# A graph network on one core: one wait a step for TensorE, relayed by ScalarE, and 32-bit step words

## The chip, the cores and the metric

The kernel runs on one core of one Trainium2 chip. The metric is the device time of one execution in microseconds. A core has TensorE (matmuls), VectorE, ScalarE and GpSimd for work on tiles, SyncE for transfers, and 16 DMA engines. In the profile they are PE, DVE, ACT, POOL and SP; a trailing q (PEq, PEldq, DVEq, SPq) marks the engine's instruction stream, that is waits, register work and DMA issues.

## What is computed

6250 nodes with 256 features, 100000 edges sorted by destination. Two blocks, each with a layer norm, a relu and a residual: a graph convolution of three hops, then a graph attention of two layers with four heads.

```python
h = relu(layernorm(x))
for i in range(3):                       # hops
    h = h * out_norm[:, None]
    h = segment_sum(h[src], dst, N)      # 100000 rows of 256 floats
    h = (h * in_norm[:, None]) @ W[i] + b[i]
    if i < 2: h = relu(h)
x = x + h
h = relu(layernorm(x))
for layer in range(2):                   # attention, with a loop edge at every node
    alpha = leaky_relu(a_src[src] + a_dst[dst])
    w = exp(alpha - segment_max(alpha, dst)[dst])
    h = segment_sum(w * h[src], dst) / segment_sum(w, dst)[dst] + bias
x = x + h
```

## The kernel before

The edges, in order of destination, are cut into EC = 782 chunks of 128. The nodes are cut into NT = 49 tiles of 128. A *step* is one chunk for one tile of destinations; a chunk that reaches into the next tile is used in two steps, so there are S = 832 steps. Which chunk and which tile belongs to a step depends on the data and is worked out on the chip at the start: `step_tab` holds, for each step, four 16-bit words: how many chunks must have arrived (ARRIVALS), the place of the chunk in the ring (SLOT_AT), the place of the tile's sums (SUMS_AT) and of its logits (LOGITS_OF). The helper `step_values` loads some of them into an engine's registers (the profile puts these loads on L363).

One hop is a pipeline of four engines, each with its stream of instructions in fixed order:

- GpSimd issues one indirect DMA for each chunk (L695), 128 rows of 1 KB from `conv_tab` into one of U = 64 slots of `ring`. Chunk c may go out when the step c - 15 has been multiplied (`products_done`, L694).
- SyncE waits for the chunks in order and counts them in `arrived` (L484, in `landed`).
- VectorE, in step s, makes the one-hot matrix of the step s + 3 from `dloc` (L1413, 128x128 f32, four buffers), then waits for the product of step s and adds it to the tile's sums in `acc` (L1421, in `accumulate`).
- TensorE, in step s, waits for the one-hots, for the add that frees the PSUM bank (four of them) and for the arrival of the chunk, and multiplies one-hot by rows (L1127). The fp32 matmul is two passes, with two records each of weight load and matmul. The two loads of eight words each, chunk counts and slots, stand ahead of every eighth step.

After a hop TensorE, ScalarE and VectorE multiply by W[i], and SyncE stores the next table. ScalarE has nothing to do within a hop, save that in hop 1 it sends the keys and the start and end flags of segments, which attention needs later, to DRAM and back (L805 to L817) while VectorE works on them in `flag_work`.

Attention goes over the same steps in groups of 16. TensorE and VectorE load sixteen words a group with `step_values`, and `accumulate` is shared with the hops.

## Time and profile before

| | |
|---|---|
| median of 3 runs | 6875.43 us (6857.97 to 6877.12) |
| the profiled execution | 6875.32 us, its span 6873.5 us |
| mean granted TensorE clock | 0.71 |
| TensorE busy (matmul) | 4202.8 us, 61% |
| VectorE busy | 3621.6 us, 53% |
| ScalarE busy | 2136.3 us, 31% |
| GpSimd busy | 4130.3 us, 60% |
| DMA | 625.46 MB, mean 91 GB/s |

Busy counts tile work alone; register loads and waits are not in it. The mean of a matmul record is modelled. An idle time that the profile puts on "issue" ended with nothing that it can name, and "remote" is a signal whose sender it does not know.

### The profile page before, as it was taken

How to read it: one execution, taken by the hardware profiler on the slowest of the kernel's cores; microseconds unless marked ns; L12 is line 12 of the kernel's file. 1: busy time of each engine (PE TensorE's matmuls, PEld its weight loads, DVE VectorE, ACT ScalarE, POOL GpSimd, SP SyncE). 2: the span in 40 equal slices, each digit the busy share in tenths (PEclk: the TensorE clock that was granted, in tenths of full speed). 3: DMA queues.
4: the chain of work that ended last, by engine and by line, in shares of the span. 5: the costliest groups of instructions: out<-in, count | busy, mean ns of one | idle time of the engine just before them, and what ended most of it. 6: DMA issues, size and time to landing. Idle time of an engine off the chain costs nothing. (4 is left out here: it accounts for less than half of the span.)

```text
span 6873.5 us, 84355 instructions
## 1 busy us (share of the span) xinstructions
PE 4202.8 (61%) x14997; PEld 2812.5 (41%) x14997; DVE 3621.6 (53%) x12180; ACT 2136.3 (31%) x7094; POOL 4130.3 (60%) x4276
## 2 busy tenths in 40 slices
PE   8555555565555556555555636666666556666774
PEld 7333333343333334333333424444444334444442
DVE  6444444544444444444444636666666556666667
ACT  4000000020000002000000247677777467767774
POOL 7666666366666664666666356566664556666663
PEclk7666666776666668666666867777778777777776
DMA  3333333133333332333333233333333323333334
GB/s 100 95 95 89 91 91 91 55 103 90 91 89 91 90 90 85 90 91 90 91 91 90 85 112 88 87 90 89 88 90 86 104 77 89 88 89 87 89 89 133
DMA packets 309602, 625.46 MB, mean 91 GB/s; under 512 B 85343, under 2 KB 180411, under 8 KB 309080
## 3 DMA queue, kind: packets, MB, share of 16 engines
q0 software_dynamic: 192928, 530.18, 27.7%
q1 hardware_dynamic: 109800, 88.51, 4.1%
q8 instruction: 167, 2.74, 0.2%
q10 hardware_dynamic: 6384, 1.39, 0.1%
q14 instruction: 323, 2.65, 0.1%
HBM read 573.23 MB, written 47.33 MB: 90 GB/s over the span
## 5 line engine op out<-in xcount | busy, mean ns | idle before, releaser
L1127 PE MATMUL main<-ring,oh 128*128 x4992 | 2039.7, 573 | 1582.9 <-DVE oh L1413 775.2
L695 POOL DMA_INDIRECT ring<-conv_tab,csrc x2346 | 2221.4, 947 | 1232.7 <-issue 613.0
L1421 DVE TENSOR_TENSOR acc<-acc,main 128x264 f32 (+2 forms) x4160 | 1762.7, 424 | 1964.9 <-PE main L1127 688.1
L1127 PEld LDWEIGHTS main<-ring,oh 128*128 128x128 f32 x4992 | 1337.3, 286 | 2282.1 <-issue 2038.2
L707 POOL DMA_INDIRECT ring<-attn_tab,sidx x1664 | 1586.1, 953 | 1079.4 <-issue 441.2
L1230 PE MATMUL main<-ring,oh 128*128 128x264 f32 x3328 | 1367.9, 528 | 354.8 <-ACT ring L959 190.5
L1413 DVE TENSOR_SCALAR oh<-iota,dloc 128x128 f32<-128x128 f32 x2505 | 765.0, 306 | 474.1 <-issue 327.2
L959 ACT ACTIVATE ring<-ring 128x64 f32<-128x64 f32 x3328 | 906.5, 340 | 0.0
L1230 PEld LDWEIGHTS main<-ring,oh 128*128 128x128 f32 x3328 | 672.9, 247 | 546.0 <-issue 349.0
L937 ACT ACTIVATE oh<-iota,dloc 128x128 f32<-128x128 f32 x1664 | 527.2, 391 | 2.7 <-DMA attn_tab<-oh 2.7
L1766 DVE TENSOR_TENSOR ring<-ring 128x128 f32<-128x128 f32 x1664 | 463.6, 284 | 0.0
L925 ACT CAST ohT_room<-pso 128x512 bf16<-128x512 f32 x416 | 241.2, 580 | 566.3 <-remote 389.9
L873 ACT ACTIVATE nb<-acc,stat 128x256 f32<-128x256 f32 x49 | 24.5, 500 | 1209.7 <-DVE stat L1520 1209.7
L859 ACT ACTIVATE nb<-acc,inorm 128x256 f32<-128x256 f32 x49 | 24.3, 498 | 1209.7 <-DVE acc L1421 1209.4
L1150 PE MATMUL pso<-ident,oh 128*128 128x128 f32 x1664 | 360.2, 356 | 39.4 <-issue 31.2
L795 ACT ACTIVATE sdeg<-sdeg 128x49 f32<-128x49 f32 x1 | 0.2, 245 | 1210.2 <-DVE sdeg L1476 1210.2
L1164 PE MATMUL psad<-tvb,ohT_room 128*128 x1664 | 275.0, 193 | 141.2 <-issue 88.8
L1164 PEld LDWEIGHTS psad<-tvb,ohT_room 128*128 128x128 bf16 x1664 | 193.8, 116 | 291.3 <-issue 211.0
L945 ACT ACTIVATE oh<-oh,ones 128x512 f32<-128x512 f32 x416 | 296.0, 712 | 0.8
L1150 PEld LDWEIGHTS pso<-ident,oh 128*128 128x128 f32 x1664 | 241.2, 182 | 74.4 <-issue 47.6
L1794 DVE TENSOR_TENSOR acc<-acc,resc 128x256 f32 x104 | 44.4, 427 | 354.0 <-issue 354.0
L1191 PE MATMUL psb<-ident,mrow 64*128 64x64 f32 x104 | 30.2, 291 | 260.6 <-DVE mrow L1714 244.6
(215 smaller groups left out, 3012.1 us busy)
## 6 DMA issues: line engine op xcount, KB each, us to landing
ring<-conv_tab,csrc POOLq DMA_INDIRECT x2346
ring<-attn_tab,sidx POOLq DMA_INDIRECT x1664
ring<-attn_tab SPq DMA_DIRECT2D x14, 896.0 KB, 8.2
conv_tab<-oh SPq DMA_DIRECT2D x12, 896.0 KB, 4.0
flag_room<-start_rows SPq DMA_DIRECT2D x416, 8.0 KB
flag_room<-end_rows SPq DMA_DIRECT2D x416, 8.0 KB
x_tab<-acc SPq DMA_DIRECT2D x7, 896.0 KB
oh<-x_tab SPq DMA_DIRECT2D x7, 896.0 KB
```

Source lines behind the costliest of these rows:

```text
L695: pool.indirect_dma_start(ring3[:, c % U, 0:C], None, conv_tab[k], bass.IndirectOffsetOnAxis(ap=csrc[:, c:c + 1], axis=0)).then_inc(gather ...
L707: pool.indirect_dma_start(ring3[:, j, 0:TW], None, attn_tab[l], bass.IndirectOffsetOnAxis(ap=sidx[:, i * GB * G + j:i * GB * G + j + 1], a ...
L937: sq = nc.scalar.activation(oh[:, (at + k) * P:(at + k + 1) * P], iota[:, :], ACT.Square, scale=-1.0, bias=dloc[:, col(k)])
L945: nc.scalar.activation(o4, o4, ACT.Relu, scale=-1.0, bias=ones[:, 0:1]).then_inc(quads_ready, 1)
L959: nc.scalar.activation(r, r, ACT.Copy, scale=ring3[:, b * G + k, C + h:C + h + 1]).then_inc(weighted_a, 1)
L1127: nc.tensor.matmul(main[s % 4][:, 0:width], oh[:, (s % OHR) * P:(s % OHR + 1) * P], ring[:, bass.ds(slots[s % 8], width)], start=True, sto ...
L1150: mm = nc.tensor.transpose(pso[q % 2][:, k * P:(k + 1) * P], oh[:, at * P:(at + 1) * P], ident[:, :])
L1164: mm = nc.tensor.matmul(psad[:, j * LW:(j + 1) * LW], ohT[:, ((q % 2) * 4 + k) * P:((q % 2) * 4 + k + 1) * P], tvb[:, bass.ds(tiles[j], LW ...
L1230: nc.tensor.matmul(main[k % 4][:, 0:AW], oh[:, (b * G + k) * P:(b * G + k + 1) * P], ring3[:, b * G + k, :], start=True, stop=True).then_i ...
L1413: return nc.vector.tensor_scalar(oh[:, at * P:(at + 1) * P], iota[:, :], dloc[:, col], None, ALU.is_equal).then_inc(onehots, 1)
L1421: nc.vector.tensor_tensor(a, a, main[k][:, 0:width], ALU.add).then_inc(added, 1)
L1766: nc.vector.tensor_tensor(r, r, w.to_broadcast([P, DVEC // CH, CH]), ALU.mult).then_inc(weighted_v, 1)
```

## The change

- `step_tab` is split. The chunk counts stay 16 bits wide (`arrival_tab`); slots, sums and logits places are 32 bits wide (`step_tab`, three rows). SyncE stores and loads two tables in place of one, and VectorE makes two copies from PSUM.
- ScalarE gets `relay_steps(k)` for each hop. For each step it waits for the one-hots and for the arrival of the chunk and increments `step_ready`. It loads the counts, four at a time.
- TensorE waits for `step_ready` alone, and loads slots alone.
- VectorE makes the one-hot of step s + 3 only when the add of step s - 1 has completed (it waited for the product of s - 1), so that a one-hot also stands for a free PSUM bank; the wait for that add ahead of the next add goes.
- The key and flag transfers of hop 1 are issued from within the relay, at steps 64, 72 and 168.

```diff
-        step_words = dram("step_words", (4, SX), U16)
+        arrival_words = dram("arrival_words", (1, SX), U16)
+        step_words = dram("step_words", (3, SX), I32)
...
-        step_tab = flag_room[H * G:H * G + 4, 0:SX // 2].bitcast(U16)
+        arrival_tab = flag_room[H * G:H * G + 1, 0:SX // 2].bitcast(U16)
+        step_tab = flag_room[H * G + 1:H * G + 4, 0:SX].bitcast(I32)
...
+        def arrivals_of(engine, s):
+
+            return nc.values_load_multi_w_load_instructions(
+                arrival_tab[0:1, s:s + 4], engines=[engine], min_val=1, max_val=EC,
+                skip_runtime_bounds_check_because="chunk counts are clamped on the chip")[1]
...
             sp.wait_ge(words_ready, 2)
-            sp.dma_start(step_words.rearrange("w (b p) -> (w b) p", p=P), step_rowsT).then_inc(words_in, 16)
-            sp.wait_ge(words_in, 16)
+            sp.dma_start(arrival_words.rearrange("w (b p) -> (w b) p", p=P), arrival_rowsT).then_inc(words_in, 16)
+            sp.dma_start(step_words.rearrange("w (b p) -> (w b) p", p=P), step_rowsT[SB:4 * SB, :]).then_inc(words_in, 16)
+            sp.wait_ge(words_in, 32)
+            sp.dma_start(arrival_tab, arrival_words).then_inc(words_in, 16)
             sp.dma_start(step_tab, step_words).then_inc(words_in, 16)
...
+            def neighbour_keys(s):
+
+                kv = keys[0:1, 0:SX * P].rearrange("o (b p e) -> (o p) b e", p=P, e=P)
                 kn = keys[0:1, 2:SX * P + 2].rearrange("o (b p e) -> (o p) b e", p=P, e=P)
+                with nc.allow_non_contiguous_dma(reason="one element of each step"):
+                    if s == SROW_AT:
+                        act.wait_ge(keys_ready, 1)
+                        nc.scalar.dma_start(keys[0:1, 1:1 + SX * P].rearrange("o (b p e) -> (o p) b e", p=P, e=P),
+                                            key[:, :, 1:P + 1]).then_inc(key_out, 16)
+                    if s == SROW_AT + 8:
+                        act.wait_ge(key_out, 16)
+                        nc.scalar.dma_start(key[:, :, 0:1], kv[:, :, 0:1]).then_inc(key_out, 16)
+                        nc.scalar.dma_start(key[:, :, P + 1:P + 2], kn[:, :, P - 1:P]).then_inc(key_out, 16)
+                    if s == EROW_AT + 56:
+                        act.wait_ge(flags_ready, 1)
...
+                    if s == S - 1:
+                        act.wait_ge(key_out, 112)
...
+            def relay_steps(k):
+
+                if k == 0:
+                    act.wait_ge(words_in, 64)
+                    act.nop(nofuse=True)
+                for s in range(S):
+                    if s % 4 == 0:
+                        counts = arrivals_of(mybir.EngineType.Activation, s)
+                    act.wait_ge(onehots, oh_base(k) + s + 1)
+                    act.wait_ge(arrived[k], counts[s % 4])
+                    act.sem_inc(step_ready, 1)
+                    if k == 0:
+                        neighbour_keys(s)
...
                 for s in range(0, S):
                     if s % 8 == 0:
-                        counts = step_values(mybir.EngineType.PE, ARRIVALS, s, 8)
                         slots = step_values(mybir.EngineType.PE, SLOT_AT, s, 8)
-                    pe.wait_ge(onehots, oh_base(k) + s + 1)
-                    pe.wait_ge(added, k * S + s + 1)
-
-                    pe.wait_ge(arrived[k], counts[s % 8])
-                    pe.nop(nofuse=True)
+                    pe.wait_ge(step_ready, k * S + s + 1)
...
+            link(nc.vector.tensor_copy(arrival_rowsT, psb[0:SB, P:2 * P]))
             nc.vector.tensor_copy(step_rowsT, psb[0:4 * SB, P:2 * P]).then_inc(words_ready, 1)
...
             def accumulate(at, k, width, s):
 
-                dve.wait_ge(products_done, CR + s + 1)
-                dve.wait_ge(added, 4 + s)
                 a = acc[:, bass.ds(at, width)]
...
-                    dve.wait_ge(products_done, CR + k * S + s)
+                    dve.wait_ge(added, 4 + k * S + s)
                     onehot(bass.ds(s + AHEAD, 1), (s + AHEAD) % OHR)
+                    dve.wait_ge(products_done, CR + k * S + s + 1)
                     accumulate(sums_at[s % 8], s % 4, C + 1 if k == 0 else C, k * S + s)
...
                         def add(k):
+                            dve.wait_ge(products_done, CR + s0 + k + 1)
+                            dve.wait_ge(added, 4 + s0 + k)
                             accumulate(sums_at[k], k % 4, AW, s0 + k)
```

## Rows read from the trace of the kernel before

**Rows 1.** The page's busy times; the chain that ended last, by line.

```profile
PE 4202.8 (61%) x14997; PEld 2812.5 (41%) x14997; DVE 3621.6 (53%) x12180; ACT 2136.3 (31%) x7094; POOL 4130.3 (60%) x4276
...
by line: PE main L1230 3.5%; issue 2.2%; another core or an unknown queue 1.6%; DVE acc L1421 1.4%; DVEq L363 1.0%; ACT ring L959 1.0%; PE pso L1150 0.8%; ACT oh L937 0.6%; DVE ring L1766 0.5%; ACT ohT_room L925 0.4%; ACT oh L945 0.3%; DVE
```

**Rows 2.** Windows of hops: length, busy PE, PEld, DVE, ACT, POOL, clock, DMA; their sum.

```profile
164.60:1371.40 1206.80, 679.64 (x1678) 446.94 (x1678) 553.05 (x1698) 0.00 (x0) 741.91 (x782) 0.67 0.31 87
...
sum 3616.70, PE 2040.74 PEld 1340.16 DVE 1621.07 ACT 0.03 POOL 2221.37; mean PE 680.25 PEld 446.72 DVE 540.36 ACT 0.01 POOL 740.46
```

**Rows 3.** Line L695, hop 1 and last row of hop 3: ns, first and last start.

```profile
L695 POOL DMA_INDIRECT ring<-conv_tab,csrc x782: 940/946/1624, 164.6 to 1305.7; - x196
...
  issue: 200.3, 598
  PE main L1127: 140.1, 151
  remote: 59.7, 32
...
L695 POOL DMA_INDIRECT ring<-conv_tab,csrc x782: 940/946/1187, 2700.7 to 3837.8; - x196
```

**Rows 4.** Timeline in hop 2: start, us, instruction, idle before it.

```profile
2010.40 0.94 POOL L695 DMA_INDIRECT ring<-conv_tab,csrc  x1 [0.30 <-issue]
...
2016.50 0.42 DVE L1421 TENSOR_TENSOR acc<-acc,main 128x256 f32 x1 [3.60 <-remote]
2017.11 0.94 POOL L695 DMA_INDIRECT ring<-conv_tab,csrc  x1 [3.27 <-remote]
```

**Rows 5.** Line L1127 in hop 1: what ended TensorE's idle time.

```profile
  issue: 888.0, 383
...
  SPq L484: 49.1, 17
```

**Rows 6.** TensorE's stream in four quiet steps; timeline of a matmul burst.

```profile
L1124 PEldq EVENT_SEMAPHORE  x4: 51/51/51, 2002.2 to 2003.2; - x4
...
901.39 4.65 PE L1127 MATMUL main<-ring,oh 128*128 x10 [2.39 <-DVE oh L1413]
```

**Rows 7.** Line L363, register loads: hop 1 (eight words), then attention (sixteen).

```profile
L363 PEldq TENSOR_LOAD <-flag_room x208: 15/1917/5031, 161.8 to 1363.5; - x104
L363 DVEq TENSOR_LOAD <-flag_room x104: 1822/1827/3355, 178.6 to 1363.4; - x104
...
L363 DVEq TENSOR_LOAD <-flag_room x104: 3582/3587/3621, 4081.3 to 6795.6; - x104
```

**Rows 8.** Lines L1124 and L1125: single records in a stretched place.

```profile
L1124 PEldq EVENT_SEMAPHORE  x1: 711/711/711, 2012.8 to 2012.8; - x1
L1125 PEldq EVENT_SEMAPHORE  x1: 699/699/699, 2014.2 to 2014.2; - x1
```

**Rows 9.** Lines L1421 (hop 1) and L484: the other engines' control records.

```profile
L1421 DVEq FUSED_REGOPS  x832: 46/46/46, 180.8 to 1370.9; - x167
L484 SPq EVENT_SEMAPHORE  x2346: 5/17/1395, 178.9 to 3841.1; - x196
```

**Rows 10.** Timeline of VectorE in a burst.

```profile
2019.22 0.42 DVE L1421 TENSOR_TENSOR acc<-acc,main 128x256 f32 x1
2019.56 0.32 DVE L1413 TENSOR_SCALAR oh<-iota,dloc 128x128 f32<-128x128 f32 x1
2019.84 0.42 DVE L1421 TENSOR_TENSOR acc<-acc,main 128x256 f32 x1
```

**Rows 11.** Timeline of ScalarE in hop 1, first and last of its DMA issues.

```profile
261.64 0.39 ACTq L805 DMA_DIRECT2D keys<-oh  x1
266.62 0.37 ACTq L810 DMA_DIRECT2D oh<-keys  x1
...
414.07 1.58 ACTq L817 DMA_DIRECT2D end_any<-oh  x1
```

**Rows 12.** Line L458: the table's transfer to SBUF.

```profile
L458 SPq DMA_DIRECT2D flag_room<-step_words x1: 247/247/247, 41.8 to 41.8; - x1
```

More of the change, by code:

```diff
@@ L250, in gnn @@
         cmpo = endt[:, 0:SB * NT].rearrange("p (b t) -> p b t", t=NT)
-        step_rowsT = oh[0:4 * SB, o_k + 3 * SX:o_k + 3 * SX + P // 2].bitcast(U16)
+        arrival_rowsT = tmp[0:SB, 0:P // 2].bitcast(U16)
+        step_rowsT = oh[0:4 * SB, o_k + 3 * SX:o_k + 3 * SX + P].bitcast(I32)
         step_cols = oh[:, o_k + 3 * SX + P:o_k + 3 * SX + P + 4 * SB]
@@ L290, in gnn @@
         flags_ready = sem("flags_ready")
-        flags_out = sem("flags_out")
+        step_ready = sem("step_ready")
         words_T = sem("words_T")
@@ L363, in step_values @@
             return nc.values_load_multi_w_load_instructions(
-                step_tab[row:row + 1, s:s + n], engines=[engine], min_val=1 if row == ARRIVALS else 0, max_val=LAST_AT[row],
-                skip_runtime_bounds_check_because="chunk, slot and tile are clamped on the chip")[1]
+                step_tab[row - 1:row, s:s + n], engines=[engine], min_val=0, max_val=LAST_AT[row],
+                skip_runtime_bounds_check_because="slot and tile are clamped on the chip")[1]
+        def arrivals_of(engine, s):
+            return nc.values_load_multi_w_load_instructions(
+                arrival_tab[0:1, s:s + 4], engines=[engine], min_val=1, max_val=EC,
+                skip_runtime_bounds_check_because="chunk counts are clamped on the chip")[1]
         ONES_COL = C
@@ L802, in _ @@
             copy_projected(NT - 1)
-            act.wait_ge(keys_ready, 1)
-            nc.scalar.dma_start(keys[0:1, 1:1 + SX * P].rearrange("o (b p e) -> (o p) b e", p=P, e=P),
-                                key[:, :, 1:P + 1]).then_inc(key_out, 16)
-            with nc.allow_non_contiguous_dma(reason="one element of each step"):
-                act.wait_ge(key_out, 16)
+            def neighbour_keys(s):
                 kv = keys[0:1, 0:SX * P].rearrange("o (b p e) -> (o p) b e", p=P, e=P)
-                nc.scalar.dma_start(key[:, :, 0:1], kv[:, :, 0:1]).then_inc(key_out, 16)
@@ L811, in _ @@
                 kn = keys[0:1, 2:SX * P + 2].rearrange("o (b p e) -> (o p) b e", p=P, e=P)
-                nc.scalar.dma_start(key[:, :, P + 1:P + 2], kn[:, :, P - 1:P]).then_inc(key_out, 16)
-                act.wait_ge(flags_ready, 1)
-                nc.scalar.dma_start(start_rows.rearrange("(b p) e -> p b e", p=P), b3(sfr)).then_inc(flags_out, 16)
-                nc.scalar.dma_start(end_rows.rearrange("(b p) e -> p b e", p=P), b3(efr)).then_inc(flags_out, 16)
-                nc.scalar.dma_start(start_any.rearrange("o (b p) -> (o p) b", p=P), sany).then_inc(flags_out, 16)
@@ L817, in _ @@
[L817 to L818 removed]
+                with nc.allow_non_contiguous_dma(reason="one element of each step"):
[9 more added lines that the diff above has]
+                        act.wait_ge(flags_ready, 1)
+                        nc.scalar.dma_start(start_rows.rearrange("(b p) e -> p b e", p=P), b3(sfr)).then_inc(key_out, 16)
+                        nc.scalar.dma_start(end_rows.rearrange("(b p) e -> p b e", p=P), b3(efr)).then_inc(key_out, 16)
+                        nc.scalar.dma_start(start_any.rearrange("o (b p) -> (o p) b", p=P), sany).then_inc(key_out, 16)
+                        nc.scalar.dma_start(end_any.rearrange("o (b p) -> (o p) b", p=P), eany).then_inc(key_out, 16)
+                    if s == S - 1:
+                        act.wait_ge(key_out, 112)
@@ L859, in rectify_scaled @@
                 nc.scalar.activation(nb_of(t), sums_of(t), ACT.Relu, scale=inorm[:, t:t + 1]).then_inc(nb_ready, 1)
+            relay_steps(1)
             act.wait_ge(added, 4 + 2 * S)
@@ L874, in rectify_centred @@
                                      ).then_inc(nb_ready, 1)
+            relay_steps(2)
             rectify_centred(0)
@@ L1114, in conv @@
                 if k == 0:
-                    pe.wait_ge(words_in, 32)
+                    pe.wait_ge(words_in, 64)
                     pe.nop(nofuse=True)
@@ L1369, in _ @@
                 scale_rows(q)
-            dve.wait_ge(words_in, 32)
+            dve.wait_ge(words_in, 64)
             dve.wait_ge(rowsT_read, KB)
```

3 lines of the change are left out of this document (1 added, 2 removed).

## The prediction, made blind

> **What bounds the kernel now.** I read the page first [rows 1]. No engine is busy for more than 61% of the span, so no engine's arithmetic is the bound; the three hops take 3616.7 us of 6873.5, their windows being the first row gather to the last add of each [rows 2]. The reader is to see that the three hops cost the same (1206.8 us the first, 1205.6 the mean) and that ScalarE does nothing in them.
>
> Next, the gathers by themselves [rows 3]. One takes 0.946 us of GpSimd, and in running order the next one starts 1.25 us after it (0.30 us "issue" between two) [rows 4]. Left alone, 782 gathers would begin within 781 x 1.25 = 976 us. They take 1305.7 - 164.6 = 1141 us, 165 us more, and the idle rows say for whom: TensorE's products, by which the gather engine is told that a ring slot is free, and "remote", which by its place in the timeline is the same wait [rows 3, 4]. After the last gather, 65.7 us more pass until the last add (1371.4): up to 48 steps are still queued. Both, 165 and 66 us, mean that TensorE lags behind the gathers. A hop would be GpSimd's, and is TensorE's.
>
> Then TensorE itself. Its array is busy 680 us of 1207 and has gaps behind "issue" (888 us before weight loads) [rows 2, 5], so it is its instruction stream that is late. In a quiet stretch the stream needs 0.33 us a step: three control records (the wait for arrivals at L1124, the waits for one-hots and adds at L1125, the address arithmetic at L1127), about 0.11 us each with the gaps (three steps between 2002.2 and 2003.2) [rows 6]. Every eighth step it loads sixteen 16-bit words into registers by two loads of 1.917 us each [rows 7]: 3.84 us per eight steps, 104 x 3.84 = 399 us a hop. And there is something stranger: in places these same 51 ns records take 0.7 us each with 0.7 us between them, so that from 2011.5 to 2016.5 two steps pass where fifteen could; VectorE waits 3.6 us and the gather engine 3.3 us in that place [rows 4, 8]. If I take the loads from the 888 us of "issue" idle, up to 489 us a hop are left for such stretches and for small gaps. The records of VectorE in the same hops show no such stretching (46 ns at the least, middle and most) [rows 9].
>
> **The change, part by part.** (a) *One load instead of two on TensorE.* 104 x 1.92 = 200 us of its stream a hop go. (b) *One wait a step.* L1124 and L1125 go, the wait on `step_ready` should ride on the address arithmetic, as VectorE's does at L1421. That is 2 x 0.11 x 832 = 175 us of the stream a hop, and control records fall from 3.25 to 1.125 a step. (c) *The stretched records.* They are seen where TensorE issues 3.25 control records in 1207/832 = 1.45 us, or 2.2 a microsecond. I expect them to follow the number of such records and to shrink to a third or go; the bounds are 0 and all 489 us kept.
>
> What the stream needs afterwards: 832 x 0.12 = 100 us + 200 us of loads = 300 us, with every stretched record kept 789 us. Both are under 976. The array: ten matmul records in 4.65 us [rows 6], at most 0.93 us a step, thus 774 us a hop, at a mean granted clock of 0.67. Even the array time and an entirely exposed load, 8 x 0.93 + 1.92 = 9.4 us for eight steps, just meet the gathers' 8 x 782/832 x 1.25 = 9.4 us.
>
> (d) *ScalarE's relay.* It lies in the chain now: one-hot and arrival, ScalarE, TensorE. No row of before shows it. The nearest are SyncE's record at L484, which is also a wait and an increment, 17 ns [rows 9], and TensorE's 0.11 us a record; two records a step make 0.2 us at most, below it is about 0.05. I take 0.2. Its loads of four words are 1.917/2 = 0.96 us per four steps, so it is busy 832 x (0.2 + 0.24) = 366 us a hop, far from being the bound. Behind its wait stand only later relays, and the root and the rectifying that open the next stage, which waited for the hop's end anyway. A one-hot is made three steps ahead, so the relay's 0.2 us lies under two or three steps of slack (1.175 us each at the gathers' pace); if that cover were gone it would cost 832 x 0.2 = 166 us. It cannot help: no gain.
>
> (e) *VectorE.* The one-hot now waits for the add before it to complete (0.42 us), where it began 0.34 us after that add's start [rows 10]. An add therefore comes every 0.62 us today and every 0.7 to 0.8 us after; eight of them plus the register load of 1.83 us make at most 8 x 0.8 + 1.83 = 8.2 us, under 9.4. Cost 0, covered by the gathers; uncovered, up to 832 x 0.16 = 133 us a hop. The separate `added` wait (21 ns) merges away, which is no gain in a chain that waits for products.
>
> (f) *The key and flag DMAs* move into the relay of hop 1. One issue at step 64, two at 72, four at 168, of 0.37 us (the second) to 1.58 (the seventh and longest) [rows 11]: under 4 x 1.58 = 6.3 us in one place, once. The wait at 72 is for a transfer whose issue and next issue are 5.0 us apart today (261.6 to 266.6), against eight steps = 9.4 us. VectorE wants the neighbours at step 96, 24 steps after their issue; the flags are wanted in attention. Gathers of some 15 steps' reserve cover each single pause. On ScalarE's queue nothing else stands. SyncE gets one store and one load more (the load 0.25 us today) and VectorE one copy; the table is sent at 41.8 us and first read at 161.8, so 120 us of other work lie over them [rows 7, 12]: 0. Without that cover they would cost a few transfers of 3 us, once.
>
> (g) *32-bit words.* Eight 16-bit words take 1.83 us on VectorE, sixteen 3.59 [rows 7]: so much a word and no fixed part. No 32-bit load is in the trace. Upper bound: the same, since the count of registers is the same. Lower: the load takes as long as one word (0.22 us). I take the same. In the hops it hardly matters, as gathers bound them. In attention it would: VectorE's load is 1.0% of the span in the chain that ended last, 69 us, and that chain reaches back over the second layer only [rows 1]; so two layers hold 138 us, and the lower bound saves 15/16 of it, 130 us.
>
> The Trainium skill bears on (g). Its page "DMA: Bandwidth & Descriptors", section "Latency and other measured facts", gives a `tensor_load` a floor of about 600 ns that loads of several values amortize. The rows show no floor for 16-bit words; if the rule is that of 32-bit words, rival B is what it does here. By the page's own figure, an estimate is (3.59 - 0.6)/3.59 x 138 = 115 us.
>
> **The sum.** A hop afterwards: 976 us of gathers, then 3.3 us until the last has landed (3837.8 to 3841.1 today) [rows 3, 9] and about 2 us for matmul and add, 982; I add 13 us for holds that stay (a twelfth of today's 165), 995. Three hops are 2985 in place of 3616.7, a gain of 632 us. The profiled run's own time is 6875.3 (span 6873.5 and 1.8 around it; the median of the runs is 6875.4, so nothing is to be corrected). 6875.3 - 632 = 6244 us.
>
> **Rivals.** *B, cheap 32-bit loads:* hops as above, and the loads in attention shrink by half or more, 69 to 130 us: about 6145. For it: the loads are on the chain. Against it: cost goes by the word in every row.
>
> *C, the stretched records move to ScalarE.* Only the engine that waits on a register's value (L1124) shows them, and that wait goes to ScalarE, with 2.25 records in 1.175 us = 1.9 a microsecond, hardly less than 2.2. Pauses of 5 us every fourteen steps would then stand ahead of TensorE, which regains them only at 0.93 us a step against 1.175: per fourteen steps 5 + 11 x 0.93 + 1.75 x 1.92 = 18.6 us if the loads are exposed, 15.3 if covered, 16.4 from the gathers. Halfway between 16.4 and 18.6, 1.25 us a step, 1040 us; with the worst end 1105. A saving of 300 to 500 us: about 6475.
>
> *D, slower.* As C, while TensorE keeps its own as well, because they come by time or by step and not by control record. Then a hop is 1207 - 200 - 175 + 489 = 1321 us if nothing overlaps, and slower than before as soon as ScalarE's pauses pass 375 us a hop. With a third of the excess overlapped, 1283: 6875 + 3 x 76 = 7103. Against it: VectorE and SyncE pass as many steps without one.
>
> *E, TensorE's stream was not what held the gathers*, but the landing of the rows, which the change leaves. Then nothing changes, 6875. Against it: TensorE waits only 49 us a hop for arrivals (the SPq row) [rows 5].
>
> **How the numbers follow.** The forecast 0.58, B 0.20, C 0.15, D 0.04, E 0.03. Forecast and B lie between 6100 and 6320, C between 6320 and 6600. The range 6110 to 6480 leaves out B's lower end (0.05), half of C and D and E: about 0.2. What a measurement can tell is about 0.3%, 21 us; D is slower, 0.04, of E and the ends of C and D 0.02 are the same, and the rest, 0.94, is faster.
>
> **What would show it.** Right: the gathers of each hop begin within 980 to 995 us and have no idle for TensorE's products but in the first fifteen; the last add comes under 10 us after the last gather; TensorE's waits name ScalarE's relay or the arrivals; 312 loads on TensorE in the hops, 624 on ScalarE of about 0.96 us; DVE's adds are 0.7 to 0.8 us apart in bursts. B: 32-bit loads under 1 us for eight words. C: ScalarE's records with a longest of 0.7 us or more in numbers, and gathers still held. The forecast is wrong if a tail of 60 us stays behind the last gather, for then TensorE or its relay is still the slower one.

## The result, and the profile after

| | before | after |
|---|---|---|
| median | 6871.9 us (4 runs, 6857.97 to 6877.12) | 6716.1 us (4 runs, 6706.15 to 6716.32) |
| ratio | | 0.977, 95% interval 0.9755 to 0.979 |
| profiled span | 6873.5 us | 6714.4 us |
| mean granted TensorE clock | 0.710 | 0.729 |

The kernel became 156 us faster. The forecast was 632 us, and 6716 lies above its range (6110 to 6480).

First the page of the kernel after: busy times, and the chain that ended last, by engine. They answer to [rows 1].

```profile
PE 4098.0 (61%) x14997; PEld 2607.9 (39%) x14997; DVE 3695.6 (55%) x12181; ACT 2132.1 (32%) x7094; POOL 4138.8 (62%) x4276
...
PE 38%; DVE 18%; issue 18%; another core or an unknown queue 14%; ACT 8%; DVEq 2%; ACTq 0%; DMA 0%; SPq 0%; POOL 0%; POOLq 0%
```

The chain is now TensorE, VectorE and time without a named reason; GpSimd has no share in it. Next the windows of the hops, from first gather to last add, with columns as in [rows 2]: hop 1, hop 3 and the sum.

```profile
163.12:1338.28 1175.16, 648.78 (x1678) 384.17 (x1678) 575.78 (x1698) 0.00 (x0) 742.38 (x782) 0.68 0.32 89
...
2633.39:3799.58 1166.19, 661.64 (x1664) 388.17 (x1664) 560.38 (x1673) 0.00 (x0) 740.81 (x782) 0.69 0.32 92
sum 3511.43, PE 1953.97 PEld 1151.10 DVE 1693.32 ACT 0.00 POOL 2224.44; mean PE 651.32 PEld 383.70 DVE 564.44 ACT 0.00 POOL 741.48
```

The three hops take 3511.4 in place of 3616.7 us, 105 less. The two attention layers, from first to last add, fell from 1269.6 and 1272.2 to 1248.6 and 1250.1 us, 43 less. Of the remaining 11 us of the spans' 159, 9 lie just ahead, between the first gather of each attention layer and its first add (111 us before, 106 and 107 after). So nearly all of the gain lies where rows are gathered.

The gathers of hop 1 at their new line, L706, answer to [rows 3].

```profile
L706 POOL DMA_INDIRECT ring<-conv_tab,csrc x782: 940/946/1653, 163.1 to 1291.4; - x196
...
  issue: 188.1, 590
  PE main L1156: 105.9, 138
  remote: 92.9, 53
```

They begin within 1128 us (1141 before, 976 forecast), and the last add comes 47 us after the last of them starts (66 before, 5 forecast). GpSimd still waits for TensorE's products. Now the records that the change was to alter: TensorE's one control record a step with its idle time behind "issue" over the three hops, the two engines' loads of 32-bit words (all stages; the median is that of eight), and ScalarE's relay and its loads of four 16-bit words.

```profile
L1156 PEldq FUSED_REGOPS  x2496: 37/37/42, 177.4 to 3797.1; - x192
...
  issue: 3305.9, 2035
...
L366 PEldq TENSOR_LOAD <-flag_room x416: 587/592/1677, 160.3 to 6603.7; - x139
L366 DVEq TENSOR_LOAD <-flag_room x416: 593/598/1481, 177.1 to 6639.8; - x139
...
L868 ACTq EVENT_SEMAPHORE  x2496: 38/38/7384, 177.3 to 3797.1; - x192
...
L372 ACTq TENSOR_LOAD <-flag_room x624: 879/884/2170, 159.8 to 3794.6; - x156
```

One control record a step is left, and none is stretched (42 ns the longest). Eight 32-bit words load in 0.59 us, where eight 16-bit words took 1.92 on TensorE and 1.83 on VectorE [rows 7]. The two waits and the increment of the relay are a single record of 38 ns, in place of the two records I had counted. But TensorE's idle time behind "issue" is 1102 us a hop, where it was 888 [rows 5].

So nearly everything that the change was to do, it did, and yet GpSimd is held. The timeline of hop 2 shows by what.

```profile
1590.12 0.30 PEld L1156 LDWEIGHTS main<-ring,oh 128*128 128x128 f32 x2 [1.93 <-issue]
...
1592.74 0.42 DVE L1449 TENSOR_TENSOR acc<-acc,main 128x256 f32 x1 [2.81 <-remote]
...
1593.68 1.22 PE L1156 MATMUL main<-ring,oh 128*128 x2 [2.86 <-issue]
...
1597.66 0.42 DVE L1449 TENSOR_TENSOR acc<-acc,main 128x256 f32 x1 [4.18 <-remote]
...
1598.61 1.21 PE L1156 MATMUL main<-ring,oh 128*128 x2 [3.71 <-issue]
1601.87 0.42 DVE L1449 TENSOR_TENSOR acc<-acc,main 128x256 f32 x1 [3.46 <-remote]
...
1602.48 0.94 POOL L706 DMA_INDIRECT ring<-conv_tab,csrc  x1 [3.26 <-remote]
1602.53 0.42 DVE L1449 TENSOR_TENSOR acc<-acc,main 128x256 f32 x1
```

The product of the matmul pair recorded from 1593.68 to 1594.90 reaches VectorE only at 1597.66, 2.8 us after its modelled end; the next pair begins at 1598.61. GpSimd at last waits 3.26 us. This is the place of [rows 4, 8] again. There the control records of a step were 0.7 us long, now none is, and the time stands between records. The adds shown begin at 1592.74, 1597.66 and 1601.87: steps of 4.9 and 4.2 us. I call such places slow groups. I count their steps as gaps of over 2 us between the starts of two adds. Most of these gaps are multiples of 0.7 us, from 2.1 to 5.6 us, before the change (before_again: 326 of the 368 in three hops that hold no register load of TensorE) and after it (after_again: 462 of 510). Fewer control records did not make a step in such a place reliably shorter: with no load in them the gaps over 2 us average 3.2 us before (before_again) and 3.3 after (after_again).

### The profile page after: what moved, and what is told of

The parts are those of the page before. It is cut to its first block, busy times and chain, and to the rows that moved or that the text cites. A ratio compares the mean times of both kernels' runs of the same rounds, so it can differ in the third digit from the quotient of the medians.

```text
span 6714.4 us, 79679 instructions
## 1 busy us (share of the span) xinstructions
PE 4098.0 (61%) x14997; PEld 2607.9 (39%) x14997; DVE 3695.6 (55%) x12181; ACT 2132.1 (32%) x7094; POOL 4138.8 (62%) x4276
## 3 DMA queue, kind: packets, MB, share of 16 engines
q10 hardware_dynamic: 6384, 1.39, 0.1%
## 4 chain that ended last, share of the span: by engine, by line
PE 38%; DVE 18%; issue 18%; another core or an unknown queue 14%; ACT 8%; DVEq 2%; ACTq 0%; DMA 0%; SPq 0%; POOL 0%; POOLq 0%
PE main L1156 21%; DVE acc L1449 9%; PE main L1259 9%; ACT ring L993 3%; PE main L1080 3%; DVE oh L1443 3%; ACT oh L971 2%; PE pso L1179 2%; DVE ring L1795 1%; ACT ohT_room L959 1%; DVE ring L1311 1%; DVEq L366 1%; ACT oh L979 1%; PE pso L1072 1%
## 5 line engine op out<-in xcount | busy, mean ns | idle before, releaser
L706 POOL DMA_INDIRECT ring<-conv_tab,csrc x2346 | 2224.4, 948 | 1187.0 <-issue 586.4
L1156 PE MATMUL main<-ring,oh 128*128 x4992 | 1953.0, 538 | 1563.4 <-issue 1076.9
L1156 PEld LDWEIGHTS main<-ring,oh 128*128 128x128 f32 x4992 | 1148.7, 259 | 2365.5 <-issue 2229.0
L1259 PE MATMUL main<-ring,oh 128*128 128x264 f32 x3328 | 1350.5, 518 | 353.9 <-DVE ring L1795 129.1
L1259 PEld LDWEIGHTS main<-ring,oh 128*128 128x128 f32 x3328 | 657.6, 242 | 565.3 <-issue 262.0
L1443 DVE TENSOR_SCALAR oh<-iota,dloc 128x128 f32<-128x128 f32 x2505 | 789.8, 316 | 150.8 <-issue 34.0
L698 POOL TENSOR_SCALAR acc<-binit,sdeg 128x256 f32<-128x256 f32 x98 | 90.4, 922 | 114.0 <-DVE tmp L1512 58.4
```

What stands on the lines that cost most here:

```text
L706: pool.indirect_dma_start(ring3[:, c % U, 0:C], None, conv_tab[k], bass.IndirectOffsetOnAxis(ap=csrc[:, c:c + 1], axis=0)).then_inc(gather ...
L1156: nc.tensor.matmul(main[s % 4][:, 0:width], oh[:, (s % OHR) * P:(s % OHR + 1) * P], ring[:, bass.ds(slots[s % 8], width)], start=True, sto ...
L1259: nc.tensor.matmul(main[k % 4][:, 0:AW], oh[:, (b * G + k) * P:(b * G + k + 1) * P], ring3[:, b * G + k, :], start=True, stop=True).then_i ...
L1443: return nc.vector.tensor_scalar(oh[:, at * P:(at + 1) * P], iota[:, :], dloc[:, col], None, ALU.is_equal).then_inc(onehots, 1)
```

## The experiments

The runs were taken in sets, each with runs of the kernel before beside it, and times of different sets are compared only through these. In the set of the result and in four others the kernel before took 6860 to 6929 us; in two it took 5619 us. I call these the first and the second condition. The traces give no name for what differs; the number of the chip does not tell them apart, since chip 8 shows both. Runs without an interval below are single executions (quartergather: two); before_third is one too.

A hop is given as above, and "span of the gathers" is from the first to the last start. Short diffs are against the kernel after.

**words16**, 16-bit slots and tiles again, with the relay kept.

```diff
-        step_words = dram("step_words", (3, SX), I32)
+        step_words = dram("step_words", (3, SX), U16)
...
```

> The changed kernel with slots, sums and logits places 16 bits wide again, all else kept (relay included). The changed kernel's register loads were 0.59 us for eight 32-bit words and 1.10 us for sixteen, where before eight 16-bit words took 1.83 to 1.92 and sixteen 3.59 to 3.79. Theory W, the word width made the gain: the time goes back by 100 to 156 us, to 6815 to 6875. Theory R, the relay and the shorter stream on TensorE made the hops' part (105 us) and the width only attention's (52 us): 6755 to 6780, with hops still near 1170 us. Loads of eight words should read 1.83 us on VectorE and 1.92 on TensorE again.

Measured: 6784.4 us beside 6859.8, ratio 0.988 (0.9858 to 0.9907); hops 1180, 1183 and 1183 us, attention 1261 and 1267. The 32-bit words alone are worth 1.1% in the first condition (1.3% in the repetition below, where all four kernels ran in one set).

**norelay**, TensorE waits by itself; 32-bit words kept.

```diff
-                    pe.wait_ge(step_ready, k * S + s + 1)
+                        counts = nc.values_load_multi_w_load_instructions(
+                            arrival_tab[0:1, s:s + 8], ...)[1]
+                    pe.wait_ge(onehots, oh_base(k) + s + 1)
+                    pe.wait_ge(arrived[k], counts[s % 8])
+                    pe.nop(nofuse=True)
...
```

> The changed kernel without the relay: TensorE waits for the one-hots and for the arrival by itself (seven instructions of its own a step in place of five) and loads eight 16-bit counts again; 32-bit words kept. Theory R: 6790 to 6830, the hops back near 1205 us. Theory W: 6716 to 6760, the hops at 1170 to 1185 us. If TensorE slows to 0.7 us for every instruction in recurring groups whatever the instruction is, its control records are stretched again, as before the change, and a step within a group takes 7 x 0.7 = 4.9 us in place of 5 x 0.7 = 3.5.

Measured: 6755.6 us, ratio 0.984 (0.9817 to 0.9868); hops 1186 to 1188. The relay with TensorE's shorter stream is worth 0.7%. From norelay to the changed kernel one wait record a step and one load of 1.92 us in eight steps go, some 290 us of TensorE's stream, and a hop falls by 16 us.

**narrow**, matmuls of 64 columns in place of 256; each product's other columns keep old values.

```diff
-                    nc.tensor.matmul(main[s % 4][:, 0:width], oh[...],
-                                     ring[:, bass.ds(slots[s % 8], width)], start=True, stop=True)
+                    nc.tensor.matmul(main[s % 4][:, 0:64], oh[...],
+                                     ring[:, bass.ds(slots[s % 8], 64)], start=True, stop=True)
```

> The changed kernel, with the matmuls of the hops cut to 64 of 256 columns (it leaves out three quarters of each product; the adds are 256 wide and so read old sums, and the degree column is not made). The number of TensorE's instructions is the same, the work of the array falls to about a third. Theory A, the slow groups follow the array's work and the rise of the granted clock: the clock stays at its lower level in the hops, the groups vanish, a hop falls to 980 to 1000 us and the kernel to 6150 to 6250. Theory N, they follow the number of TensorE's instructions: the groups stay, every 14 to 16 steps, and a hop stays at 1120 to 1170 us. Theory G, they follow the gathers' traffic: as N.

**onepass**, the upper 16 bits of one-hots and rows, read in place as bf16 (so rows are cut to bf16), so that a matmul is one record.

```diff
...
-                                      ring[:, bass.ds(slots[s % 8], width)], start=True, stop=True)
+                                      ring_b[:, bass.ds(slots[s % 8], width, 2)], start=True, stop=True)
```

> The changed kernel, with the matmuls of the hops in one pass on the upper halves of the fp32 words, read as bf16 (one-hots stay exact, rows are cut to bf16). TensorE issues three instructions a step in place of five, and the array works half as long or less. Theory N: the groups come every 24 steps or so and a step in one takes 3 x 0.7 = 2.1 us, a hop falls to 1000 to 1060 us. Theory A: the groups vanish, a hop is 980 to 1000 us. Theory G: the groups keep their distance of some 20 us, only their steps are shorter, a hop is 1050 to 1100 us.

Measured: narrow 6699.3 us, onepass 6667.7 us, both beside 6859.8. The windows of hop 1, narrow first:

```profile
163.91:1332.01 1168.10, 516.44 (x1678) 408.37 (x1678) 567.06 (x1698) 0.00 (x0) 743.79 (x782) 0.50 0.32 90
```

```profile
165.10:1321.31 1156.21, 319.30 (x846) 89.43 (x846) 537.57 (x1698) 0.00 (x0) 743.18 (x782) 0.50 0.32 91
```

Array time falls to 516 and 319 us and hop 1 by 7 and 19 us; narrow's other two hops (1172 and 1166 us) are as long as the changed kernel's. The granted clock is at its lower level (0.50, thus 1.2 GHz) all through both, and the slow groups are there, in narrow with 714 us of gaps over 2 us in hop 2 (680 in after). Neither the array's work nor the steps of its clock makes them.

**filler**, one more matmul a step, of two columns, into an unused bank.

```diff
+                    nc.tensor.matmul(psb[:, 0:2], ident[:, :], ident[:, 0:2], start=True, stop=True)
```

> The changed kernel, with one more fp32 matmul of two columns after each step of a hop, into a PSUM bank that nothing reads: four more TensorE instructions a step (nine in place of five) and hardly more work of the array. Theory N: the slow groups come after 8 to 9 steps in place of 15, a step in one takes 9 x 0.7 = 6.3 us, and a hop grows by 30 to 60%, to 1500 to 1850 us; the kernel to 7700 to 8700. Theory A: the groups keep their places, but their steps are longer; a hop of 1250 to 1400 us. Theory G: as A.

Measured: 6955.8 us beside 6929.0; hops 1219, 1249 and 1248. The mean hop is 1239 us, 68 more than after's, of which about 10 are the slower set (1% on the kernel before). This isn't the 0.7 us for each instruction that the expectation tested: nine instructions a step would make gaps of 6.3 us, and only three gaps over 5.7 stand in three hops. In hop 2 the gaps over 2 us are fewer (165 in place of 202) and take 575 us in place of 680; the 666 other steps cost 1.00 us each in place of 0.77.

**nogather**, hops without row gathers: GpSimd only counts chunks as arrived, and the ring keeps its first filling.

```diff
-                    pool.indirect_dma_start(ring3[:, c % U, 0:C], None, conv_tab[k], ...
-                                            ).then_inc(gathered[c % U], 16)
+                    pool.sem_inc(arrived[k], 1)
```

> The changed kernel without the row gathers of the hops: GpSimd, still held by the products, counts a chunk as arrived at once (all rows are ones, the 2346 gathers and their traffic are left out). Theory G, the gathers' traffic makes the slow groups: they vanish, and a hop takes 832 x 0.93 = 775 us or less. Theories N and A: the groups stay or come sooner, since TensorE is now never fed too slowly; a hop of 1050 to 1200 us.

Measured: 4949.0 us beside 6929.0. The sum over the hops:

```profile
815.79:1373.28 557.49, 479.58 (x1662) 265.11 (x1660) 512.71 (x1663) 0.00 (x0) 0.00 (x0) 1.00 0.01 2
...
sum 1690.54, PE 1448.31 PEld 800.31 DVE 1553.21 ACT 0.00 POOL 0.00; mean PE 482.77 PEld 266.77 DVE 517.74 ACT 0.00 POOL 0.00
```

A hop takes 557 to 572 us with the clock at its upper level, with two gaps over 2 us in all three hops. The attention layers of the same execution still gather and take 1266 and 1263 us, so this is the first condition. In it TensorE and VectorE with relay and loads are capable of 0.67 us a step; the slow groups need the gathers beside them.

**halfrow**, gathers of 512 B rows; half the columns are not brought.

```diff
-                    pool.indirect_dma_start(ring3[:, c % U, 0:C], None, conv_tab[k],
+                    pool.indirect_dma_start(ring3[:, c % U, 0:C // 2], None, conv_tab[k].rearrange('n (h c) -> (n h) c', h=2),
```

> The changed kernel, with gathers of 128 values in place of 256 (512 bytes a descriptor in place of 1 KB; the row index then meets half rows of the table, so it gathers other numbers, and the second half of a slot stays ones). The number of descriptors and GpSimd's work are the same, the bytes are half. Theory G-bytes, the transfers sustain 91 GB/s, which is 1.44 us a gather, and what exceeds it comes back as slow groups on TensorE: the groups vanish or become rare, a hop falls to 980 to 1010 us, the kernel to 6150 to 6250. Theory G-count, it is the number of descriptors or of gathers that counts: nothing changes, a hop of 1160 to 1175 us, 6690 to 6730.

**paced**, a memset of 64 columns ahead of each gather, so that no two gathers stand closer than 1.39 us.

```diff
+                    link(nc.gpsimd.memset(cslow[:, :], 0.0))
                     pool.indirect_dma_start(ring3[:, c % U, 0:C], None, conv_tab[k],
```

> The changed kernel, with a memset of 64 columns of an unused tile on GpSimd ahead of each gather of the hops, so that gathers can begin only every 1.5 us or so in place of 1.25. If the gathers' path sustains no more than one in 1.44 us on average (theory G), then with gathers slower than that the slow groups on TensorE vanish nearly, GpSimd is never held, the tail behind the last gather falls below 10 us, and a hop takes 782 x the new pace, 1170 to 1220 us: hardly more than now. If instead each gather adds its share of slow time whatever the pace, the groups stay as many per gather and a hop grows by the added 0.25 x 782 = 195 us, to 1320 to 1370 us.

Measured: halfrow 6703.5 and paced 6697.9 us, both beside 6864.3; hops 1163 to 1170 and 1158 to 1167. First the gathers of paced in hop 2, then those of halfrow.

```profile
L708 POOL DMA_INDIRECT ring<-conv_tab,csrc x782: 951/951/1067, 1388.5 to 2511.4; - x196
```

```profile
L706 POOL DMA_INDIRECT ring<-conv_tab,csrc x782: 938/945/1016, 1391.2 to 2510.7; - x196
```

Gathers that may follow each other at 1.25 us begin within 1120 us, and gathers that may only do so at 1.39 us within 1123. With gaps joined that stand under 3 us apart, paced has 21 to 32 groups a hop of 756 to 776 us in all, against 59 to 65 of 668 to 687 in after: fewer and longer. Halving the bytes or spreading the gathers doesn't remove them, and the average stays at 1.44 us a gather.

**actnops**, ten empty instructions of ScalarE behind each relay; **halfgather**, gathers of 64 rows (the other 64 partitions keep their first filling); **onepass_timed**, onepass once more, in 11 runs.

```diff
                     act.sem_inc(step_ready, 1)
+                    for _ in range(10):
+                        act.nop(nofuse=True)
```

```diff
-                    pool.indirect_dma_start(ring3[:, c % U, 0:C], None, conv_tab[k],
-                                            bass.IndirectOffsetOnAxis(ap=csrc[:, c:c + 1], axis=0)
+                    pool.indirect_dma_start(ring3[0:P // 2, c % U, 0:C], None, conv_tab[k],
+                                            bass.IndirectOffsetOnAxis(ap=csrc[0:P // 2, c:c + 1], axis=0)
```

> The changed kernel, with ten no-operations on ScalarE after each step's signal in the hops: 8320 control instructions a hop that nothing waits for, on an engine that is idle two thirds of the time. Theory Q, one path shared by all engines and the transfers sets the pace, each instruction and each packet taking its share (from the gathers' spans of onepass, after, before and filler against the number of instructions in a hop, 0.011 us an instruction): the gathers' span in a hop grows by 8320 x 0.011 = 94 us, to 1220, and the kernel to about 6970 to 7020. Theory T, only TensorE's own instructions and the gathers meet: no change, 6690 to 6740, unless the relay itself is late, by at most 0.5 us a step in bursts.

> The changed kernel, with gathers of 64 rows in place of 128 (half of the descriptors and of the bytes in each of the same 782 gathers; the upper 64 rows of each slot stay ones). If the pace of one gather in 1.44 us belongs to descriptors, the slow groups vanish and a hop falls to the larger of GpSimd's pace for such a gather and TensorE's 0.65 to 0.93 us a step: 700 to 900 us, the kernel 5300 to 5900. If it belongs to the gather as such, a hop stays at 1160 to 1175 us.

> The kernel onepass again, timed in rounds, as the fastest version so far that computes the whole (rows cut to bf16 in the hops' matmuls): 6660 to 6680 us, a ratio of 0.970 to 0.974 to the kernel before.

Measured: 5614.1, 5524.3 and 5608.8 us, beside a kernel before of 5618.7 us (15 runs, 5613.4 to 5625.5). The unchanged kernel was 1240 us faster than in the fastest earlier set. onepass stood at 0.9984 of it (0.9975 to 0.9993), where it had been at 0.972. actnops' hops are 984 us, halfgather's 953, onepass' 983. None of the three tells what it was made for, since the slow groups are not there to be changed.

**before_again, after_again, norelay_again, words16_again** are unchanged copies, in one set.

> The kernel before, unchanged, once more with its trace. The last three kernels ran beside a before of 5619 us where all earlier ones had 6860 to 6929. If the slow groups (0.7 us for each TensorE instruction, several steps long) are a condition of the chip on which a run falls, then in a run near 5620 us they are absent from the kernel before too, a hop is 980 to 1010 us and the gathers begin 1.25 us apart; in a run near 6860 us they are there and a hop is 1207 us. If the fast times have another reason (bytes, loads), the groups are there in both.

> The changed kernel, unchanged. Theory one (the 489 us a hop were a condition of the chip, and without it a hop is the gathers' own 976 us with or without the change): beside a before of about 5620 us the change is worth under 1%, its hops 982 to 995 us as the prediction summed them; beside a before of about 6865 us the ratio is 0.977 again. Theory two (the change gains in attention by cheaper loads of 32-bit words in either condition): 20 us a layer, some 40 us in all, even beside 5620 us, ratio 0.993.

> TensorE waits by itself for one-hots and arrivals, 32-bit words kept. Beside a before of about 5620 us: the same as the changed kernel within 0.3% if the gathers bound the hops there, since both streams fit under 1.25 us a step; slower by over 0.5% if the relay matters. Beside a before of about 6865 us: 0.984 again, slower than the changed kernel by 0.6%.

> The changed kernel with 16-bit words, so loads of 1.9 us for eight in place of 0.6. Beside a before of about 5620 us: the same as the changed kernel in the hops, and in attention up to 20 us a layer more if the loads of VectorE lie in its chain there as well, so 0 to 0.7% slower than the changed kernel. Beside a before of about 6865 us: 0.988 again.

Measured: the first condition again. Before 6870.6 us (15 runs), its copy at 1.0004 (0.9994 to 1.0014), after 6712.0 at 0.977 (0.9757 to 0.9785), norelay 6759.0 at 0.984 (0.9825 to 0.9857), words16 6799.8 at 0.990 (0.9885 to 0.9917). Every ratio of the first sets came back.

**quartergather, after_third, before_third**: gathers of 32 rows, and two unchanged copies.

> Each gather of the hops brings 32 rows in place of 128; the other 96 partitions of the ring keep their first filling, so the results are other numbers. All instructions of TensorE and VectorE stay. Beside a before of about 6865 us: if the slow groups come from the descriptors and rows that the queue moves, a quarter of them lets the average gather come every 1.25 to 1.3 us and the hop falls under 1050 us; if they go with the count of instructions or of gathers, the pace stays at 1.43 to 1.44 us and the hop at 1165 to 1170 us. Beside a before of about 5620 us: the gather itself is shorter (0.91 us for 64 rows), so a hop of 930 to 955 us.

> The changed kernel once more, for the chip that this call falls on. Beside a before of about 6865 us: ratio 0.977, the third time. Beside a before of about 5620 us: hops of 982 to 986 us, and a ratio of 0.997 to 1.000, since the gathers bound every hop with and without the change.

> The kernel before, for its trace. Beside a before of about 6865 us: hops of 1204 us with some 90 slow groups each, as twice before. Beside a before of about 5620 us: no slow groups but the code loads of TensorE, hops of 985 to 1010 us, the gathers 1.25 us apart.

Measured: the second condition. Before 5619.1 us (13 runs, 5614.0 to 5622.4); after 5616.9, ratio 0.9996 (0.9987 to 1.0006); quartergather 5438.7, 0.968. The change is worth nothing here that can be told from zero. The windows of the hops in before_third: hop 2 and the sum.

```profile
1212.08:2199.19 987.11, 615.38 (x1664) 448.27 (x1664) 536.75 (x1664) 0.00 (x0) 741.30 (x782) 0.75 0.37 105
...
sum 2957.84, PE 1829.14 PEld 1322.01 DVE 1637.42 ACT 0.00 POOL 2223.31; mean PE 609.71 PEld 440.67 DVE 545.81 ACT 0.00 POOL 741.10
```

And of after_third, the sum:

```profile
sum 2952.44, PE 2304.29 PEld 1098.03 DVE 1865.64 ACT 0.00 POOL 2220.84; mean PE 768.10 PEld 366.01 DVE 621.88 ACT 0.00 POOL 740.28
```

The unchanged kernel's hop is 986 us, the changed one's 984. The next rows are of the kernel before in the second condition: its gathers and what ended GpSimd's idle time (hop 2), its waits for arrivals at L1124 (all hops), its register loads (hop 1).

```profile
L695 POOL DMA_INDIRECT ring<-conv_tab,csrc x782: 942/946/1017, 1212.1 to 2190.4; - x196
...
  issue: 164.2, 539
  PE main L1127: 73.7, 242
...
DMA to landing us min/median/max: 2.6/2.8/4.9
...
L1124 PEldq EVENT_SEMAPHORE  x2496: 51/51/51, 179.0 to 3243.7; - x192
...
L363 PEldq TENSOR_LOAD <-flag_room x208: 1915/1918/5142, 161.9 to 1140.9; - x104
```

781 gathers in 978.3 us are 1.253 us each, as in [rows 4], with 0.30 us between two whoever is named (164.2 + 73.7 = 238 us of 782 gaps). The loads are as dear as ever; no wait of L1124 is over 51 ns. The timeline shows how TensorE pays for its stream without the hop paying:

```profile
2001.00 6.50 PE L1127 MATMUL main<-ring,oh 128*128 x16 [3.46 <-DVE oh L1413]
...
2002.36 0.94 POOL L695 DMA_INDIRECT ring<-conv_tab,csrc  x1 [0.30 <-PE main L1127]
...
2009.86 0.95 POOL L695 DMA_INDIRECT ring<-conv_tab,csrc  x1 [0.30 <-issue]
2011.00 0.93 PEld L1127 LDWEIGHTS main<-ring,oh 128*128 128x128 f32 x3 [3.90 <-issue]
```

Eight steps (16 matmul records) run in 6.5 us, then TensorE stands for 3.5 us and loads words, and the gathers pass through it at 1.25 us. GpSimd may run 15 chunks ahead of TensorE at the least, some 19 us, so that single pauses don't reach it, and in the kernel before, too, the whole of the stream that (a) and (b) removed fits into the gathers' time: only 8 steps are still queued when the last gather starts, where in the first condition there are 64 to 66.

In quartergather the gather is shorter, and the hop follows:

```profile
L706 POOL DMA_INDIRECT ring<-conv_tab,csrc x782: 867/872/930, 1153.7 to 2072.8; - x196
```

(2072.8 - 1153.7)/781 = 1.177 us, the 0.872 us of the instruction and 0.30. With 0.908 us in halfgather it was 1.213, with 0.946 it is 1.25. In the second condition GpSimd's time for one gather is the hop.

## Why the prediction was wrong

**The step that failed** is the sum of TensorE's stream after the change, built on (c): "with every stretched record kept 789 us. Both are under 976." It takes the unexplained 489 us as a fixed amount that goes with the control records, and adds it to the shorter stream alone. The runs show three things in its place.

First, it didn't go. Control records fell from 3.25 to 1.125 a step and the groups stayed, with the time moved from the waits to the places between weight loads and products.

Second, it wasn't fixed. In the prediction's own terms, idle behind "issue" less loads, 888 - 399 = 489 us became 1102 - 61 = 1041 us a hop, though part of this now is waiting under that name (after_third has about 545 by the same count in hop 1, when gathers bound it). The gaps between adds tell it better. I take hop 2 and split the gaps over 2 us by whether TensorE begins a register load in them (moved 0.6 us ahead, since the load runs ahead of the add):

| hop 2 | gaps over 2 us with a load | without a load | the other steps |
|---|---|---|---|
| before_again, first condition | 99, 349 us | 125, 396 us | 607, 453 us |
| after_again, first condition | 35, 120 us | 167, 561 us | 629, 482 us |
| before_third, second condition | 104, 423 us | 0 | 727, 557 us |
| after_third, second condition | 0 | 12, 29 us | 819, 947 us |

The change did take away the pauses of the loads, 229 us of them. The slow groups, the column without a load, grew by 165 us and ate most of it. If a load is given to a gap when it overlaps it, the slow groups go from 346 to 579 us, which says the same. In the second condition the kernel before has all its load pauses and not one slow gap in this hop.

Third, the groups don't run beside the array's work, and 789 us left that out. With the slow groups kept at 396 us, the 120 us with loads, and the 671 steps that remain at 0.77 us each, a hop is some 1030 us, an estimate from this table: already above 976. The growth makes it 1163, and so GpSimd waits.

The premise at the end of the third paragraph, that TensorE lags because "it is its instruction stream that is late", was at most a small part of the cause. In the second condition the same stream of the same kernel holds the gathers for 2 us a hop, not 165, and leaves 7 to 9 us behind the last gather's start, not 66. In the first condition a shorter stream did help, by 35 us a hop.

**Why a sum from one trace missed it.** The 489 us were a remainder, not a count: idle time less loads. The kernel before as run in the second condition has neither the stretched records nor the excess, with every instruction in place. The hop that the prediction summed, 995 us, is 11 us from what both kernels take there (986 and 984); that is no merit of the change, which gains 2 us a hop.

**Point by point.** (a) The second load went, and the rest got cheaper too. (b) The wait rides on the address arithmetic: right, one record of 37 ns. The product there is 183 us and not 175, on which nothing hangs. What norelay takes back of (a) and (b) is 16 us a hop in the first condition; in the second the whole change gives 2. Not "up to 48" but 66 steps are still queued when the last gather of hop 1 starts. (d) The relay's record takes 38 ns, less than my bounds of 0.05 to 0.2; how much later TensorE learns of a step by it was not measured. Its load took 0.88 us for the 0.96 I summed. (e) Adds in a burst begin 0.66 us apart (1601.87, 1602.53), a little under the 0.7 to 0.8; covered. (f) Nothing of it is seen in the hop that carries it: hop 1 is 9 us longer than hop 3, 3 before, so 6 us at the most (3 in the repetition). (g) was wrong by its size: I took "the same", eight words for 1.83 us, and measured 0.59.

The Trainium skill's page "DMA: Bandwidth & Descriptors", section "Latency and other measured facts", gives a `tensor_load` a floor of about 600 ns that several values share. This case's rows agree for 32-bit words (0.59 us for eight, 1.10 for sixteen, so 0.06 us for each word beyond eight) and disagree for 16-bit words, which cost 0.23 us each with no floor (1.83 for eight, 3.59 for sixteen).

**The rivals.** B had the right mechanism in its loads, at the wrong place in the sum: attention gave 43 us in the first condition, of which words16 puts some 30 on the loads (1261 and 1267 against 1249 and 1250; about 41 in the repetition), not 69 to 130; and in the second condition nothing, since each layer there is 1039 to 1041 us with and without them, 832 gathers at 1.25. B did not have the 12 us a hop that the words gain in the first condition. C has the right symptom (groups that stay and hold the gathers) and the wrong carrier: of ScalarE's 2496 records 18 are over 0.1 us, and 17 of these stand in the first 17 us of hops 2 and 3, where the first rows have yet to come. D was right that the groups come by something other than the control record, and wrong in adding a second set on ScalarE. E says that TensorE's stream was not what held the gathers. The second condition bears this out, but not E's mechanism: rows land 2.8 us after a gather starts in both conditions.

**Where the 156 us come from.** 35 us a hop, three times, and some 50 in attention. By single parts the words save 12 us a hop and 30 to 41 us in attention (words16), and the relay with TensorE's shorter stream saves 16 us a hop (norelay). These are measured in sets of their own and repeated. Why the slow groups leave just this much of the some 340 us a hop that TensorE's loads gave back is not shown. The span of the gathers in a hop hardly follows TensorE's work: in the first condition it is 1109 to 1141 us in before, after, words16, norelay, narrow, onepass, halfrow and paced, and 1165 in filler. So time saved on TensorE seems to come back as slow groups, as if something else set the average; no run isolates what.

**What stays open** is what the slow groups are. Shown: they need the gathers (nogather, and the stages between the hops take 62 us in both conditions); less array work, a clock at its lower level, half the bytes, spread gathers or fewer control records don't remove them; they belong to the set of runs and not to the kernel. Packets on the instruction queues take as long in both conditions (median 1.0 and 1.1 us for 16 KB, in before_again and before_third), so longer loading of code isn't the reason either. Not tested in the first condition: the count of rows in a gather (both runs fell in the second), idle control instructions on ScalarE (likewise), and what else was on the chip.

## What to carry to other kernels

A stall that the profile puts on "issue", and that you know only as a remainder after all counted instructions, is not yet yours to remove. Where its runs differ, compare the sum with a trace of the unchanged kernel from another time; here that showed the hop at 986 us with every instruction in place. Don't carry such a remainder over as a fixed amount: here it grew when the loads beside it shrank. Before counting pauses by the distance of an engine's results, separate those that a known instruction makes, as the register loads did here. And before pricing a shorter stream, ask whether the buffer between the engines (15 chunks of 1.25 us here) hides it already.

## What the runs showed of the hardware

- Loads from SBUF into registers: 32-bit words 0.59 us for eight and 1.10 for sixteen; 16-bit words 0.23 us each. In the second condition no hop and no attention layer shows the difference; in the first 32-bit words save 12 us a hop and 30 to 41 us in attention.
- The same kernel takes 5619 us in some sets of runs and 6860 to 6929 in others, each repeatable within 0.5%, with the same landing time of gathers (2.8 us). The clock isn't the reason: onepass has 0.50 in the hops of both, which take 1153 and 983 us. The 1250 us between them all lie in stretches with indirect gathers: 659 in the hops and 595 in attention, counted from a layer's first gather to its last add.
- In the second condition the adds still stand about 2.5 us apart some 15 times a hop (actnops, hop 2), the last add ahead of each gap 0.6 to 1.7 us after the start of a 16 KB packet on an instruction queue; onepass_timed, with fewer instructions, has 9 to 12. That looks like the loading of TensorE's code, which no run tested, and the ring hides it.
- Indirect gathers of 128, 64 and 32 rows of 1 KB follow one another at 1.25, 1.21 and 1.18 us: a quarter of the rows saves 6%.
- Two waits on different semaphores and an increment on ScalarE made one record of 38 ns.
